# A maximum's query tile takes 128 adjacent queries, and the row of shifts is written by eight transfers of single values

## What is computed

```python
enc, ca = ctx[:, :2044], ctx[:, 2044:]
hs = mha(x @ Wq, enc @ Wk, enc @ Wv)            # 8 heads, softmax over 2044 keys
ca_q1 = einsum('btc,th->bch', ca, Wq_ca)[:, indices, :]
ca_q2 = mha(ca_q1, x, x) @ Wq
ca_hs2 = mha(ca_q2, ca @ Wk_ca, ca @ Wv_ca)     # 4 keys
out = (hs + ca_hs2) @ Wout + b_out + x
```

## Time and profile before

| | |
|---|---|
| median of 3 timed runs | 1248.68 us (1245.05 to 1251.03) |
| profiled execution | 1242.7 us |
| its span, first to last instruction | 1240.9 us |
| granted TensorE clock, mean over the span | 0.994 |
| PE busy | 1222.9 us (99%) |
| DVE, ACT, POOL busy | 67%, 55%, 17% |

### The profile page before, as it was taken

The page is one execution under the profiler, slowest core; times in us unless marked ns, Lnnn a source line. Parts: engine busy times, 40 slices in busy tenths (PEclk is TensorE's granted clock), DMA queues, the critical chain, the costliest instruction groups (busy, mean ns, idle before and its releaser), DMA issues.

```text
span 1240.9 us, 14533 instructions
## 1 busy us (share of the span) xinstructions
PE 1222.9 (99%) x5652; PEld 963.0 (78%) x5652; DVE 832.9 (67%) x1162; ACT 678.5 (55%) x770; POOL 209.8 (17%) x115
## 2 busy tenths in 40 slices
PE   7999999999999999999999999999999999999998
PEld 6889888898567677777777777777777777776898
DVE  6339725681234378888878878888888887878451
ACT  6233324222544466677677677677777767778210
POOL 1100000000000011222322221221221221233233
PEclk9999999998999999999999999999999999999999
DMA  8995898896840064264254344345335425421264
GB/s 305 297 325 168 239 284 239 265 258 145 239 107 1 1 170 109 74 149 107 68 147 106 91 124 108 110 113 125 101 95 150 97 74 149 130 70 59 68 223 135
DMA packets 96575, 180.68 MB, mean 146 GB/s; under 512 B 17289, under 2 KB 50057, under 8 KB 92378
## 3 DMA queue, kind: packets, MB, share of 16 engines
q1 hardware_dynamic: 88938, 157.33, 46.3%
q0 software_dynamic: 2816, 11.80, 3.0%
q10 hardware_dynamic: 4752, 10.62, 2.5%
HBM read 116.32 MB, written 63.24 MB: 145 GB/s over the span
## 4 chain that ended last, share of the span: by engine, by line
PE 96%; DVE 2%; ACT 1%; issue 1%; DMA 0%; ACTq 0%
PE at_ps L1223 28%; PE bank L644 19%; PE at_ps L1204 18%; PE at_ps L204 9%; PE acc_t_ps L1000 7%; PE at_ps L1396 6%; PE s_ps L967 2%; PE bank L621 2%; PE bank L591 1%; PE f_ps L940 1%; PE acc_t_ps L978 1%; PE f_ps L920 1%; DVE prob_lo L1082 1%; PE f_ps L204 1%; PE f_ps L929 0%
## 5 line engine op out<-in xcount | busy, mean ns | idle before, releaser
L212 DVE TENSOR_REDUCE mpart<-at_ps 128x1 f32<-128x512 f32 x480 | 326.5, 686 | 109.4 <-PE at_ps L204 107.8
L1145 ACT ACTIVATE prob_hi<-at_ps 128x1024 fp32r<-128x1024 f32 (+1 forms) x256 | 263.2, 1028 | 199.2 <-PE at_ps L1204 199.2
L1223 PE MATMUL at_ps<-prob_hi,v 128*81 128x512 f32 (+1 forms) x1024 | 319.7, 397 | 0.2 <-issue 0.2
L1082 DVE TENSOR_TENSOR prob_lo<-probs,prob_hi 128x1024 fp32r<-128x1024 f32 (+1 forms) x209 | 268.4, 1284 | 18.9 <-ACT probs L1150 18.9
L1150 ACT ACTIVATE probs<-at_ps 128x1024 f32<-128x1024 f32 (+1 forms) x256 | 261.0, 1019 | 0.0
L1082 POOL TENSOR_TENSOR prob_lo<-probs,prob_hi 128x1024 fp32r<-128x1024 f32 x47 | 113.0, 2405 | 538.0 <-ACT probs L1150 538.0
L1223 PEld LDWEIGHTS at_ps<-prob_hi,v 128*81 128x81 f32 (+1 forms) x1024 | 154.0, 152 | 59.5 <-issue 6.6
L204 PE MATMUL at_ps<-a 128*128 128x512 f32 x480 | 194.2, 405 | 0.5 <-DVE p2g L865 0.5
L204 PEld LDWEIGHTS at_ps<-a 128*128 128x128 f32 x480 | 153.7, 320 | 32.7 <-DVE mpart L212 1.3
L1223 PE MATMUL at_ps<-prob_lo,v 128*81 128x512 f32 (+1 forms) x512 | 160.0, 394 | 4.2 <-DVE prob_lo L1082 4.2
L1204 PE MATMUL at_ps<-a 128*128 128x512 f32 (+1 forms) x512 | 161.8, 397 | 0.0
(11 more groups left out here) (140 smaller groups left out, 1436.1 us busy)
## 6 DMA issues: line engine op xcount, KB each, us to landing
v_hi_d<-v_t SPq DMA_DIRECT2D x16, 648.0 KB, 8.1
v_lo_d<-v_t SPq DMA_DIRECT2D x16, 648.0 KB, 11.7
v<-v_hi_d SPq DMA_DIRECT2D x16, 648.0 KB, 4.7
v<-v_lo_d SPq DMA_DIRECT2D x16, 648.0 KB, 5.9
k_hi_d<-out_hi SPq DMA_DIRECT2D x40, 256.0 KB, 5.3
k_lo_d<-out_lo SPq DMA_DIRECT2D x40, 256.0 KB, 6.2
a<-k_hi_d SPq DMA_DIRECT2D x16, 640.0 KB, 7.4
b<-k_hi_d SPq DMA_DIRECT2D x16, 640.0 KB, 11.3
```

The lines of the kernel that those rows point to most:

```text
L212: dve.tensor_reduce(self.mpart[:, g % 2, qt, c:c + 1], mx_ps[k % 2][:, 0:w], AX, ALU.max).then_inc(self.mx_done, 1)
L1082: eng.tensor_tensor(pl[n % PB][0:r, :], prob[n % PF][0:r, :], ph[n % PB][0:r, :].bitcast(F32), ALU.subtract).then_inc(sem, 1)
L1145: act.activation(ph[n % PB][0:r, :], s_ps[n % 2][0:r, :], ACT.Exp, scale=SCALE).then_inc(ph_done, 1)
L1223: mm = pe.matmul(o_ps[:, u * CH:(u + 1) * CH], a[0:r, t, :], y[n % PB][0:r, u * CH:(u + 1) * CH], start=t == 0 and m == 0, stop=t == KT - ...
```

## The change

The diff does two things that belong together. A query tile of the maximum now consists of queries 128 qt to 128 qt + 127, so the stationary operand of a score piece is 128 adjacent columns of `a` where it was every eighth. Column qt of `mneg` then holds 128 adjacent queries, one in each partition, and `shift` copies it with one DMA for each query tile: 128 single values into 512 adjacent bytes of the row of shifts. There are eight such DMAs a head, and the wait of PE counts all eight.

```diff
--- before.py
+++ after.py
@@ -189,8 +189,9 @@
 
         p = g % 2
         sp.wait_ge(self.neg_done, g + 1)
-        sp.dma_start(self.queries_b(g)[SHIFT:SHIFT + 1, :].rearrange("o (q g) -> o q g", q=P).bitcast(F32),
-                     self.mneg[:, p, :].bitcast(F32)).then_inc(self.neg_in[p], 16)
+        for qt in range(ST):
+            row = self.queries_b(g)[SHIFT:SHIFT + 1, qt * P:(qt + 1) * P].rearrange("o (q i) -> o q i", i=1)
+            sp.dma_start(row.bitcast(F32), self.mneg[:, p, qt:qt + 1].bitcast(F32)).then_inc(self.neg_in[p], 16)
 
     def score_piece(self, pe, mx_ps, g, k):
 
@@ -201,7 +202,7 @@
             self.a_loaded(pe, g)
         if n >= 2:
             pe.wait_ge(self.mx_done, n - 1)
-        pe.matmul(mx_ps[k % 2][:, 0:w], self.queries_a(g)[:, qt:SQ:ST], self.keys_a(g)[:, c * CH:c * CH + w],
+        pe.matmul(mx_ps[k % 2][:, 0:w], self.queries_a(g)[:, qt * P:(qt + 1) * P], self.keys_a(g)[:, c * CH:c * CH + w],
                   start=True, stop=True).then_inc(self.mx_full, 1)
 
     def max_piece(self, dve, mx_ps, g, k):
@@ -1195,7 +1196,7 @@
                 if t == 0:
                     at.a_loaded(pe, g)
                     pe.wait_ge(at.qkb_in[g % 2], (g // 2 + 1) * 64)
-                    pe.wait_ge(at.neg_in[g % 2], (g // 2 + 1) * 16)
+                    pe.wait_ge(at.neg_in[g % 2], (g // 2 + 1) * 16 * ST)
                 if n >= 2:
                     pe.wait_ge(e_done, n - 1)
                 for a, y, first in ((at.keys_a(g), at.queries_a(g), True), (at.keys_b(g), at.queries_b(g), False)):
```

## The result

| | before | after |
|---|---|---|
| median of 6 runs (least to most), us | 1247.11 (1243.29 to 1251.03) | 1289.83 (1286.32 to 1292.68) |
| span of the profiled execution, us | 1240.9 | 1284.5 |
| mean granted clock of TensorE | 0.994 | 0.984 |

The ratio is 1.0345, with a 95% interval of 1.0324 to 1.0366: the changed kernel is 42.7 us slower. The prediction had 23.3 us, and 1289.8 us lies above its range. The direction was right, the size was not. In the changed file the transfers are issued by L194, and lines behind it are one higher than before (L205 a score piece, L1205 the scores, L1224 the values).

A forecast was written before the change was run, and what follows sets the result against it. PE, busy 99% of the span, was taken to bound the kernel. Stalls of +27.1 us less 3.8 us from shorter loads made +23.3 us on the 1248.7 us median: 1272 us, range 1256 to 1282 us.

The forecast's parts named there:

- the stalls: PE's waits for the eight transfers at 15 heads' first scores: thirteen of 1.73 us, 1.90 and 2.68, together 27.1 us.
- the loads: Shorter weight loads of the attention's 480 score pieces, mostly hidden behind matmuls: 8 ns each, 3.8 us gained.
- the clock: PE's granted clock at the first scores of a head: expected still at 1.00, so nothing in the sum.
- The loads for the next head but one: On SP behind the eight transfers: 2 us later or less, wanted a whole head later, so no cost.
- the same formula of margin over pitch: Margin of 2.47 us before PE needs the row: seven more issues fit at 0.353 us or faster.
- The first head's pieces in the stage of the tokens: 32 pieces there: the fp32 matmul before sets the time, not the load, so the gain is nothing.
- the one that took 0.05 us off the pitch: Pitch of the eight issues on SP: 0.645 us from `ca<-ntop`, less 0.05, taken as 0.60 us.
- The upper bound that I had worked out: Stalls of PE at a pitch of 0.645 us: 31.8 us; with nothing gained by the loads, 1280.5 us.
- rival (c): PE's clock falls behind each of the 15 stalls, 1.7 us each: 26 us on top, 1298 us; chance 0.04.
- (a): The eight issues on SP stay hidden for all heads but the last: 1246 us; chance 0.05.
- (b): The long loads of the score pieces are exposed, shorter ones give PE 63.4 us: 1212 us; chance 0.02.
- (d): Transfers of single values land late, each microsecond costing 15 us: 1287 us for the first; chance 0.06.

The follow-up runs named there:

- e1: Kernel before with only the adjacent queries in the score pieces, still one transfer a head: 1238.27 us, ratio 0.9966 to the kernel before.
- e8: Kernel before, queries still strided, with eight transfers a head of 16 partitions and 8 values each: 1277.45 us, ratio 1.0282 to the kernel before.
- e6: Kernel before, queries still strided, row of shifts sent in six transfers: 1256.82 us, ratio 1.0117 to the kernel before.
- e7: Kernel before, queries still strided, row of shifts sent in seven transfers: 1268.20 us, ratio 1.0208 to the kernel before.
- e2: Kernel before, queries still strided, row of shifts sent in eight transfers of single values: 1286.26 us, ratio 1.0354 to the kernel before.
- e12: Changed kernel run once more, unaltered, beside others on the same chip: 1286.11 us, ratio 1.0351 to the kernel before.
- e9: Changed kernel with a head's maxima finished three tiles before its end in place of four: 1380.69 us, ratio 1.1114 to the kernel before.
- e11: Changed kernel with eight more matmuls, results overwritten, ahead of each of the 15 waits for the row of shifts: 1270.10 us, ratio 1.0218 to the kernel before.
- e10: Changed kernel with seven of the eight columns of maxima reduced, negated and sent two tiles ahead: 1238.44 us, ratio 0.9964 to the kernel before.

## Why the prediction was wrong

The sum had two terms that matter, the stalls and the loads, and a third, the clock, at nothing. The account is drawn up from the two traces, whose spans are 1284.5 - 1240.9 = 43.6 us apart:

| term | forecast, us | measured, us |
|---|---|---|
| stalls of PE | +27.1 | +34.3 |
| half clock behind them | 0 | +12 |
| slower start of the twelve matmuls behind a wait | 0 | +1.0 |
| shorter loads | -3.8 | -6.0 (by the timed runs -4.1) |
| together | +23.3 | +41.3 |

The stalls are more than the 31.9 us of the waits' row. That row counts from the end of the matmul before, and in an unbroken line the next one starts 0.16 us ahead of that end (it takes 0.40 us at a pitch of 0.233 us): 31.9 + 15 x 0.16 = 34.3. The twelve matmuls behind a wait take 2.86 us at full clock, where they took 2.79, and 4.3 to 4.4 us where the clock falls, 1.5 us more, eight times. The remaining 2.3 us lie outside the starts of heads. The trace after has two waits there that the trace before has not, of 1.9 and 1.5 us, and its long half-clock stretches ahead of and behind the attention have other lengths; they are not followed further.

**What held.** PE is the bound, and 15 of 16 rows of shifts are waited for, at the first load of a head. The strided load was hidden in the way the tiles showed: -4.1 us in the timed runs for a forecast of -3.8. The loads for the next head but one start 5 us behind the first of the eight issues, and no wait of PE is put down to them. Four transfers, by the same formula of margin over pitch, just fit. The first head's pieces in the stage of the tokens gained nothing (a matmul of theirs takes 688 ns in both kernels).

**The stalls, +7 us.** The step that failed is the one that took 0.05 us off the pitch. The rows of `ca<-ntop` had 0.645 us between issues, and I took 0.60, since a single issue of the row of shifts is 0.48 us and not 0.53. A single one says nothing of a row of them: from the second on they come every 0.644 us, in this shape too. The last is issued 4.39 us after the first, not 4.2, and lands after 2.0, not 1.9; 15 times 0.29 is 4.4 us. Another 1.3 us come because PE itself asks sooner once the loads are short: in the kernel before and in e1, neither of which waits, the first scores start 68.2 and 66.9 us after the issue, added over the 15 heads. The two halves of the change had been priced as if they did not touch. The rest is single groups of issues that took longer, the longest wait being 2.88 us in mid-attention. The upper bound that I had worked out, 31.8 us of stalls, was nearer than the forecast. The nearest row gave the figure, and correcting it with a row of another kind spoiled it.

**The clock, +12 us.** This is the larger miss. I had the mechanism as rival (c), priced it nearly right from the earlier trace rows, at 1.7 us a fall (measured: 3.4 us at half clock, and 1.5 to 1.6 us longer), and then gave it 0.04 and left it out of the sum and of the range. It came at 8 of the 15 waits, where the rival had all or none. The reason for the 0.04 was that the one fall in the trace stood behind 4.19 us and the stalls would be 1.7 us. One fall behind 4.19 us says where it does fall, not where it does not: in the attention the trace had no wait between 0.6 and 4.19 us to say more. It even had a second stretch at half clock, from 294.1 to 304.3 us in the stage of the tokens, with no wait of PE over 0.6 us in the 10 us ahead of it, which I overlooked. The price of an unknown like that belongs in the range. Whether stalls of the forecast 1.73 us would have brought falls stays open: in e8 one of 1.74 us did and one of 1.77 us did not. The runs give the falls at starts of heads by length of the stalls:

| run | typical stall, us | stretches at half clock |
|---|---|---|
| e6 | 0.6 | none |
| e7 | 1.2 | only behind the last stall, of 2.2 |
| e8 | 1.5 | 4 of 15, behind 1.7, 2.0 and 2.5 (twice) |
| e2, changed, e12 | 1.8 to 2.0 | 6, 8, 7 of 15 |
| e9 | 6.8 | 15 of 15 |
| e11, stalls full of matmuls | at most 1.0 | none |

e11 shows that the idle PE is what brings the clock down at the starts of heads. Behind the 37 stalls of at most 1.6 us in e6, e7 and e8 it never fell; behind the 53 from 1.7 to 3.2 us in e7, e8, e2, e12 and the changed kernel it fell 26 times; behind the 15 of e9 always. What decides between 488 us and 536 us, where 2.22 us brought a fall and 1.99 us did not, stays open: in the changed kernel the first six falls come at every second head, one wait of 2.88 us (the head that starts at 1015 us) brought none, and one of 1.91 us did.

**The other rivals.** (a) needed a pitch of 0.353 us, and no group of the eight issues came near it. (b) is refuted by e1: the 132 ns less a load gave 0.009 to 0.012 us. The rule of the Trainium skill (TensorE: Matmul & The Clock Gate, The mechanism) that was cited for it does not hold for full-height loads here. The same section also lets a load run ahead when it goes to the background weight buffer, which the prediction left out and with which e1 agrees. (d), a late landing, was 0.1 us of slip in the median and not a microsecond.

## What to carry to other kernels

A transfer cut into n is priced by its issues: n times the pitch of issues behind one another, taken from a row in which they do stand behind one another, against the margin up to the first wait; four fit here, and six did not. Where a cut makes PE wait, add for each wait the possible fall of the clock, some 1.5 us a time here, and put that in the range even where the trace shows no wait so short. If the parts of a transfer are ready at different times, send each when it is ready: in e10 the eight then cost nothing. And two halves of a change that are right apart need not add up: here the shorter loads made PE ask sooner for a row that came later.

## What the runs showed of the hardware

- Issues behind one another on SP, from SBUF into one partition, come every 0.644 us, while a single one takes 0.48 us and loads with long rows from DRAM come 0.46 us apart; 128 runs of 4 bytes and 16 runs of 32 bytes cost the same on SP (5.0 and 4.95 us for eight), and land 2.0 and 1.7 us after their issue.
- A weight load of 128 fp32 columns at a step of eight takes 320 ns and an adjacent one 188 ns, and behind matmuls at a pitch of 0.23 us all but 0.009 to 0.012 us of the difference is hidden (e1).
- PE's clock fell to its lower level behind stalls as short as 1.74 us (e8), mostly for 3.4 us at a time and at a cost of 1.5 us; of 53 stalls from 1.7 to 3.2 us 26 brought a fall, of 37 of at most 1.6 us none. Behind stalls of 6.8 us (e9) it stayed there longer.
- VectorE's negation of 128x8 values, 0.17 us, took 2.31 us while a pass of GpSimd of 2.40 us ran; in 14 of 14 such heads of e9 it ended 0.03 us behind the pass.
